# First stage of a LayerNorm, attention and 8-bit FFN kernel: row normalization on ScalarE, score keys on GpSimd, weights loaded once and in four buffers, column maxima after the next statistics

## The reference

```python
x: (4, 512, 512) f32
xn = layernorm(x)                                # over the last axis, no affine part
q = (xn @ wq).reshape(B, T, 32, 16); k = xn @ wk; v = xn @ wv      # one key and one value head of 16
probs = softmax(causal(q k^T / 4)); s = (probs @ v).reshape(B, T, 512) @ wo
h = linear8bit(xn, W1, b1); g = silu(linear8bit(h, W2, b2))
return x + s * g
# linear8bit: columns of x whose absolute maximum is over 3.0 go through a float product,
# the others through a product of int8-quantized rows of x and of W
```

## Time and profile before

| | us |
|---|---|
| median of 3 runs | 842.08 |
| lowest and highest | 839.84 and 845.34 |
| the profiled execution | 841.47 |
| span in its trace | 839.6 |
| PE busy | 772.8 (92%) |
| DVE busy | 664.5 (79%) |
| ACT busy | 402.7 (48%) |
| POOL busy | 255.0 (30%) |

### The profile page before, as it was taken

The page is one execution under the profiler, slowest core; times in us unless marked ns, Lnnn a source line. Parts: engine busy times, 40 slices in busy tenths (PEclk is TensorE's granted clock), DMA queues, the critical chain, the costliest instruction groups (busy, mean ns, idle before and its releaser), DMA issues. The chain is left out here.

```text
span 839.6 us, 12084 instructions
## 1 busy us (share of the span) xinstructions
PE 772.8 (92%) x4253; PEld 581.5 (69%) x4253; DVE 664.5 (79%) x1132; ACT 402.7 (48%) x682; POOL 255.0 (30%) x331
## 2 busy tenths in 40 slices
PE   2899899999999999998879999999987999998982
PEld 2687665556676676665668788787866888886772
DVE  6888899999999999885355665856469998599967
ACT  2123156676776677777424455454444332242321
POOL 7100225555555555553511011101000000136306
PEclk9999789999999999999999999999999999999997
DMA  5731212233322233335244525112005254025852
GB/s 142 248 110 51 50 40 68 81 84 80 103 79 79 81 99 89 89 105 165 77 149 153 193 96 201 45 32 87 26 12 190 62 163 126 25 78 167 273 184 100
DMA packets 53884, 89.90 MB, mean 107 GB/s; under 512 B 10288, under 2 KB 18496, under 8 KB 52416
## 3 DMA queue, kind: packets, MB, share of 16 engines
q1 hardware_dynamic: 53824, 89.13, 33.9%
HBM read 47.69 MB, written 28.31 MB: 91 GB/s over the span
## 5 line engine op out<-in xcount | busy, mean ns | idle before, releaser
L849 DVE TENSOR_REDUCE rowmax<-ps 128x2 f32<-128x512 f32 (+3 forms) x384 | 210.0, 589 | 19.7 <-PE ps L912 17.9
L773 ACT ACTIVATE probs<-ps 128x512 f32<-128x512 f32 (+1 forms) x352 | 174.6, 558 | 71.0 <-PE ps L925 69.4
L912 PE MATMUL ps<-km,stack 128*128 128x256 f32 (+3 forms) x512 | 149.7, 347 | 2.2 <-PEq L171 1.9
L925 PE MATMUL ps<-stack,ks 128*128 128x512 f32 (+1 forms) x352 | 131.6, 383 | 2.7 <-ACT probs L773 2.6
L912 PEld LDWEIGHTS ps<-km,stack 128*128 128x128 f32 (+1 forms) x512 | 94.4, 198 | 43.2 <-DVE rowmax L849 23.7
L1651 PE MATMUL ps<-big_h 128*128 128x512 f32 x256 | 101.0, 394 | 10.2 <-DVE big_l L1576 10.1
L1323 PE MATMUL ps<-big_h,w1h 128*128 128x512 f32 x256 | 105.0, 410 | 1.4 <-DVE w1l L1195 1.4
L755 POOL TENSOR_SCALAR_AFFINE_SELECT probs<-probs 128x512 f32<-128x512 f32 x128 | 80.6, 638 | 78.7 <-ACT probs L773 77.6
L1325 PE MATMUL ps<-big_h,w1l 128*128 128x512 f32 x256 | 101.6, 397 | 0.0
L1324 PE MATMUL ps<-big_l,w1h 128*128 128x512 f32 x256 | 101.3, 396 | 0.0
L1652 PE MATMUL ps<-big_l,big_h 128*128 128x512 f32 x256 | 100.4, 392 | 0.0
(11 more groups left out here) (194 smaller groups left out, 1303.1 us busy)
## 6 DMA issues: line engine op xcount, KB each, us to landing
stack<-big_h SPq DMA_DIRECT2D x128, 64.0 KB, 2.0
projected_rows<-w2t_scratch SPq DMA_DIRECT2D x32, 256.0 KB, 2.7
h_scratch<-hs SPq DMA_DIRECT2D x7, 1024.0 KB, 4.5
hload<-h_scratch SPq DMA_DIRECT2D x14, 512.0 KB, 4.8
xn_scratch<-xa SPq DMA_DIRECT2D x4, 1024.0 KB, 4.3
stack<-big_l SPq DMA_DIRECT2D x64, 64.0 KB, 2.0
xi<-xn_scratch SPq DMA_DIRECT2D x16, 256.0 KB, 2.7
xe_scratch<-xm SPq DMA_DIRECT2D x16, 256.0 KB, 2.3
```

Source lines behind the costliest of these rows:

```text
L773: nc.scalar.activation(probs[p][:, o:o + nh * w], ps[:, STB[n % NST], 0:nh * w], ACT.Exp).then_inc(s_exp, 1)
L849: nc.vector.tensor_reduce(dst, src, AX_X, ALU.max).then_inc(s_red, 1)
L912: last = nc.tensor.matmul(dst, stack[u % 3][rows, hp, P * qt:P * (qt + 1)], km[rows, u // KT, p0:p0 + npar, keys], start=True, stop=True)
L925: ins = nc.tensor.matmul(ps[:, STB[n % NST], 0:nh * w].rearrange("p (h q) -> p h q", h=nh), ks[:, u // KT, p, P * kt:P * (kt + 1)], stack[ ...
```

## The change

- ACT, not DVE, normalizes the rows of groups 1 to 3: `normalize(g+1)` is four activations `x * rstd + shift` of 128x512 behind the two copies of kv(g); DVE forms `shift = -mean * rstd` (128x4). Group 0 stays on DVE, with a signal for each tile, and PE transposes tile by tile.
- POOL, not DVE, forms `ks`: two additions of 128x512 for a group, in front of the spare rows of `km`.
- `wk` and `wv` are loaded once; ACT and DVE read `wk` six times over. Only the 16 zero columns are written by POOL.
- `wq` is loaded in four DMAs of 128x512 into four tiles that are free then, not into `xa`. SP loads group 1 right behind it and waits for nothing.
- The column maxima of group g stand behind `layernorm(g+1)` on DVE. The low parts have their own semaphore `s_tl`, on which PE's kv waits; the maxima free the banks (`s_paf`).
- q(g,1) and q(g,2) stand in front of t(g+1).

```diff
-            if g + 1 < B:
-                a_order += [("q", g, k) for k in range(1, KT)] + [("v", g, 0)]
+                a_order += [("q", g, k) for k in range(1, 3)]
                 a_order += [("t", g + 1, k) for k in range(KT)]
+                a_order += [("q", g, k) for k in range(3, KT)] + [("v", g, 0)]
...
# SP
-                sp.wait_ge(s_wkvz, 1)
-                for c in range(6):
-                    sp.dma_start(wkv_in[:, :, HD * c:HD * (c + 1)],
-                                 wk.rearrange("(k p) n -> p k n", p=P)).then_inc(s_wload["wkv"], 16)
...
-                sp.dma_start(wq_in, wq.rearrange("(k p) n -> p k n", p=P)).then_inc(s_wload["wq"], 16)
-                sp.wait_ge(s_wl, 2)
+                sp.dma_start(wk_in[:, :, :], wk.rearrange("(k p) n -> p k n", p=P)).then_inc(s_wload["wkv"], 16)
+                sp.dma_start(wv_in[:, :, :], wv.rearrange("(k p) n -> p k n", p=P)).then_inc(s_wload["wkv"], 16)
+                for k in range(KT):
+                    sp.dma_start(wq_in[k], wq[P * k:P * (k + 1), :]).then_inc(s_wq[k], 16)
                 load_rows(1)
...
# POOL
+                    for p in range(2):
+                        nc.gpsimd.tensor_tensor(ks[:, g, p, :], km[:, g, p, :].bitcast(F32),
+                                                cols[:, 4 + p:5 + p].broadcast_to([P, T]), ALU.add).then_inc(s_ks, 1)
+                    pool.wait_ge(s_ks, 2 * (g + 1))
...
# ACT
+                def normalize(g):
+                    act.wait_ge(s_sh, g)
+                    for i in range(QT * g, QT * (g + 1)):
+                        rows = xa[:, i % (2 * QT), :]
+                        nc.scalar.activation(rows, rows, ACT.Identity, bias=shift[:, i:i + 1],
+                                             scale=rstd[:, i:i + 1]).then_inc(s_xn, 1)
...
                         nc.scalar.copy(kvh.bitcast(F32R), ps[:, n % 8, :]).then_inc(s_pah, 1)
+                        if g + 1 < B:
+                            normalize(g + 1)
...
# DVE
-                        nc.vector.tensor_reduce(colmax[:, k, g:g + 1], ps[:, n % 8, :], AX_X, ALU.max,
-                                                apply_absolute_value=True)
...
+                        if k == KT - 1:
+                            if g + 1 < B:
+                                layernorm(g + 1)
+                            for j in range(KT):
+                                nc.vector.tensor_reduce(colmax[:, j, g:g + 1], ps[:, a_at[("t", g, j)] % 8, :], AX_X,
+                                                        ALU.max, apply_absolute_value=True).then_inc(s_paf, 1)
...
-                            ins = nc.vector.tensor_scalar(ks[:, g, p, :], km[:, g, p, :].bitcast(F32),
-                                                          cols[:, 4 + p:5 + p], None, ALU.add)
```

More of the change, by code:

```diff
@@ L110, in block_layernorm_attention_ffn @@
         nt_ = sp_("newton", [P, NT])
+        shift = sp_("shift", [P, NT])
         colmax = sp_("colmax", [P, KT, B])
@@ L121, in block_layernorm_attention_ffn @@
         s_x = [sem(f"x_loaded{g}") for g in range(B)]
-        s_wload = {n: sem(f"{n}_loaded") for n in ("wq", "wo", "wkv", "b1")}
+        s_wload = {n: sem(f"{n}_loaded") for n in ("wo", "wkv", "b1")}
+        s_wq = [sem(f"wq_loaded{k}") for k in range(KT)]
         s_wkvz = sem("wkv_zeroed")
@@ L287, in _ @@
                 deviation(0)
[L288 to L291, removed]
+                act.wait_ge(s_wload["wkv"], 16 * 2)
+                nc.scalar.copy(keys_of(wkvh), repeated(wk_in)).then_inc(s_wh, 1)
+                nc.scalar.copy(wkvh[:, :, 7 * HD:P], wv_in[:, :, :]).then_inc(s_wh, 1)
+                for k in range(KT):
+                    act.wait_ge(s_wq[k], 16)
+                    nc.scalar.copy(wqh[:, k, :], wq_in[k]).then_inc(s_wh, 1)
                 for kind, g, k in a_order:
@@ L340, in layernorm @@
                     step(nc.vector.tensor_tensor(rstd[:, r], rstd[:, r], nt_[:, r], ALU.mult))
[L341 to L344, removed]
+                    if g:
+                        nc.vector.scalar_tensor_tensor(out=shift[:, r], in0=mv[:, r, 0], scalar=-1.0, in1=rstd[:, r],
+                                                       op0=ALU.mult, op1=ALU.mult).then_inc(s_sh, 1)
+                    else:
+                        for i in range(QT):
+                            nc.vector.tensor_scalar(xa[:, i, :], xa[:, i, :], mv[:, i, 0:1], rstd[:, i:i + 1],
+                                                    ALU.subtract, ALU.mult).then_inc(s_xn, 1)
                 def weight_low(dst, src, hi, n):
@@ L355, in _ @@
                 layernorm(0)
-                weight_low(wkvl[:, :, :], wkv_in[:, :, :], wkvh[:, :, :], 1)
-                weight_low(wql[:, :, :], wq_in, wqh[:, :, :], 2)
+                weight_low(keys_of(wkvl), repeated(wk_in), keys_of(wkvh), 1)
+                weight_low(wkvl[:, :, 7 * HD:P], wv_in[:, :, :], wkvh[:, :, 7 * HD:P], 2)
+                for k in range(KT):
+                    weight_low(wql[:, k, :], wq_in[k], wqh[:, k, :], 3 + k)
                 for kind, g, k in a_order:
@@ L379, in _ @@
                                                          ALU.mult))
[L380 to L383, removed]
-                            ins = nc.vector.tensor_scalar(ks[:, g, p, :], km[:, g, p, :].bitcast(F32),
-                                                          cols[:, 4 + p:5 + p], None, ALU.add)
+                            ins = nc.vector.scalar_tensor_tensor(out=km[:, g, p, :], in0=kvl,
+                                                                 scalar=cols[:, 2 + p:3 + p],
+                                                                 in1=km[:, g, p, :].bitcast(F32),
+                                                                 op0=ALU.mult, op1=ALU.add)
                         ins.then_inc(s_paf, 1)
@@ L425, in three @@
                         if ready is not None:
-                            pe.wait_ge(s_paf, ready + k)
+                            pe.wait_ge(s_tl, ready + k)
                         nc.tensor.matmul(dst, lh(k), rh(k), start=(k == 0), stop=False)
@@ L435, in _ @@
                     if kind == "t":
+                        if g == 0:
+                            if k:
+                                continue
+                            for j in range(QT):
+                                pe.wait_ge(s_xn, j + 1)
+                                for f in range(KT):
+                                    last = nc.tensor.transpose(ps[:, f, P * j:P * (j + 1)], xa[:, j, P * f:P * (f + 1)],
+                                                               ident[:, :])
+                                    if j == QT - 1:
+                                        last.then_inc(s_pa, 1)
+                            continue
                         if k == 0:
-                            pe.wait_ge(s_xn, g + 1)
+                            pe.wait_ge(s_xn, QT * (g + 1))
                         for j in range(QT):
```

36 lines of the change are left out of this document (23 added, 13 removed).

## The result

| | before | changed |
|---|---|---|
| median of 4 runs each, us | 841.39 | 831.53 |
| lowest and highest | 839.84 and 845.34 | 828.53 and 832.86 |
| the profiled execution | 841.47 | 830.80 |
| its span | 839.6 | 829.0 |
| first row maximum of the second stage (DVE) | 94.51 | 81.77 |

The ratio to the kernel before is 0.9863, 95% interval 0.9835 to 0.989: faster by 1.4%. In a second series (6 runs of the changed kernel, 10 of the one before) it was 0.9851, interval 0.9817 to 0.9886. The forecast was 829.7 with a range of 825.5 to 836.

What follows compares the result with a forecast made beforehand. The first stage was taken as bound by DVE. Gains of 3.8 + 4.2 + 1.4 + 2.4 = 11.8 us off the profiled 841.47 gave 829.7 us, range 825.5 to 836.

Steps and rivals of the forecast that it cites:

- What bounds the kernel: First stage, some 94 us: bound by DVE, whose list costs 18.92 us a group where PE needs 15.86.
- Part 1, the start: Start of the first stage: kv(0) starts at 14.7 and not 18.51, 3.8 us gained, bounds 1.8 and 4.5.
- Part 2, the pause: PE's wait at 30.61 before t(1): 4.2 us go whole, and 1.4 more since PE's clock doesn't fall.
- The clock coming up earlier: Upside in kv(0): PE's clock rises earlier, up to 2.4 us, of which 2 counted, giving 827.7.
- Part 3, the steady state: Later groups of the first stage: DVE takes 16.5 us a group; PE's waits of 1.43 and 1.01 go, 2.4 us.
- the first rival: DVE and ACT's loop stays the bound, activations 0.8 us apiece, t(2) and t(3) wait: 833 us, chance 0.15.
- Part 4: Work given to POOL and ACT: nothing on the path, 0 to 1 us for what stands behind it.
- two rivals with a low clock within the stage: First stage, PE at half speed: 17.4 us long gives 838 (chance 0.08); 40 us gives 848, slower (0.04).
- the gain hidden later: Next stage waits for something that doesn't come earlier, so the whole stays at 841 us; chance 0.05.

Runs made afterwards that it cites:

- first profile: Changed kernel, its first profiled execution, full-speed start: 73.40 us from first normalized tile to first row maximum (85.36 before), span 829.0 us.
- second profile: The same changed kernel profiled again, nothing edited, half-speed start: 72.56 us from first normalized tile to first row maximum, span 828.0 us.

## Why the prediction was right, step by step

- **What bounds the kernel** held for the kernel before: what the loads took off DVE's list arrived at the end (3.7 us), and the reorder of PE's work gave nothing as long as that list was the bound. In the changed kernel DVE and PE are so close that it depends on the execution: the keys showed with their full length (3.2 us), the three normalizations with 2.6 of 5.5 us. One thing the reading left out: both distances, 18.92 and 16.35, hold 1.2 us in which DVE itself waits for ACT's two copies of kv, which ACT begins only when DVE has copied the values of the group before. No run took that out; without it DVE's list would be near 15.1 us (16.35 - 1.22, an estimate), under PE's 15.86. The rows, before and after:

```profile
49.40 0.69 DVE L376 TENSOR_TENSOR w1t_first<-projected_rows 128x512 f32<-128x512 f32 x1 [1.20 <-ACT projected_rows L305]
```

```profile
40.21 0.69 DVE L411 TENSOR_TENSOR w1t_first<-projected_rows 128x512 f32<-128x512 f32 x1 [1.22 <-ACT projected_rows L330]
```

- **Part 1, the start**, 3.8 us: kv(0) started 4.5 us earlier, of which 0.8 came from tiles of x that landed earlier in that execution. From the first normalized tile to kv(0) it is 9.36 before (18.51 - 9.15) and 5.67 after: 3.7. The loads give 3.1 of that (6.27 with them alone), the maxima behind the low parts 0.6 (6.27 again with them undone).
- **Part 2, the pause**, 4.2 + 1.4 us: it went whole. The rows of group 1 were ready at 23.2 (forecast 23.7). t(1) came at 25.01 and not 28.0 in the first profile, since kv(0) started 0.7 us earlier than forecast and ran at full speed from its first matmul (0.47 us, against 0.77); in the second profile, with the half-speed start, it came at 27.98.
- **The clock coming up earlier**, counted as up to 2 us on the good side, was worth nothing. The changed kernel was profiled with both: first part 73.40 with the full-speed start and 72.56 with the half-speed one. PE's gain was given back in front of the queries, t(2) and t(3) (0.38, 0.28, 0.89, 0.29 us), because DVE and ACT were the slower ones then. And the 0.84 us by which the full-speed start came out longer are POOL's copy: it held a DVE instruction for 1.5 us in the first profile (2.00 and not 0.49) and for 0.7 in the second (1.40 and not 0.68), and from the first tile to the statistics of group 2 it was 22.97 and 22.19 us. With the half-speed start the view marks no wait at all after the start of kv(0), and only t(3) came 0.3 us late (16.13 us behind t(2)):

```profile
15.27 0.77 PE L460 MATMUL ps<-xth,wkvh 128*128 128x512 f32 x1 [1.33 <-DVE xtl L396]
```

  This is the last row of that kernel's PE timeline that has a wait, until the second stage.
- **Part 3, the steady state**, 2.4 us: the waits of 1.43 and 1.01 went. In the first profile 1.8 us of new waits took their place, which the sum had at nothing; there the first 24 matmuls took 5.5 us and not 7.8, which it had at nothing either. That its 12.0 us meet the forecast's 11.8 is therefore partly luck; in the second profile the waits stayed away as forecast. 16.5 a group measured 16.35. An activation costs 811 ns alone and 0.71 apart (2.94 us for four); I had 0.65, from a row with a scale alone. The Trainium skill ("ScalarE: Activation LUTs", What ACT_TABLE_LOAD costs) has a fixed part that grows with each operand of one value a row, and an estimate from its figures, for two such operands and 512 elements, is 799 ns and 0.71 apart; the trace agrees, and I should have taken it as a bound. But that is only 0.2 us for four. The waits for ACT came from PE being early: the rows of t(2) were ready at 43.0, near the forecast's 42.7, and PE wanted them at 42.25 and not at 43.7. So the first rival, whose condition was 0.8 apiece, came true in its mechanism only in 1.2 us of pauses for ACT (0.89 and 0.29) with the full-speed start, of which 0.3 were left with the half-speed one; its price of 3.4 us was too high.
- **Part 4**, POOL: 1.04 us an addition where I took 1.28 to 2.24, and no one waited. What I had put at 0 to 1 us, contention with POOL, did cost DVE 1.5 and 0.7 us in the two profiles, but by an old instruction, the copy of the spare rows, which had fallen into DVE's wait for the rows of group 1 before.
- **The clock at the changes of stage**: I took the later stages as a constant. They scatter by 5 us over the twelve traces, more than any term of the sum.
- The sum of 11.8 stands against 12.0 in the first part and 12.8 against its second profile; in whole runs the medians differ by 9.9 and by 13.4 us in the two series.
- The two rivals with a low clock within the stage, and the gain hidden later, are out: the granted clock was 1.00 from 14 to 80 us, and the rest (747.2 and 745.8) isn't longer than 745.1 beyond its scatter.

```profile
14.00:80.20 66.20, 63.61 (x309) 51.76 (x309) 58.58 (x125) 29.50 (x53) 21.26 (x41) 1.00 0.32 110
```

## What to carry to other kernels

Where two engines are nearly full, compare the length of one round in each one's own list (here 18.92 against 15.86 us), not their busy shares; the longer list is the one to take work from, and a new order on the shorter gives nothing yet. Look also for waits inside the longer round. Worths of edits don't add up: the same order of products was worth nothing before and 5.8 us after, so undo parts from the changed kernel as well as trying them alone. When an experiment lands on a rival's number, follow the time through the timeline before you give the rival the mechanism; here an instruction on a third engine had eaten the difference. To weigh parts of some microseconds in a kernel of 840, measure between two events within the trace that every version has, and take the changed kernel's profile twice.

## What was not expected of the hardware

- A VectorE instruction that starts while GpSimd's copy of 32x2048 runs is held until about its end, whatever its own size: 1.82 us for a `tensor_tensor` of 128x4 that takes 0.16 (loads alone), 1.64 for one of 128x512 that takes 0.68 (order undone), 2.00 for a `tensor_scalar` that takes 0.49 (changed). The three ended 0.0, 0.6 and 0.3 us after the copy. Five more traces have the same, with 0.7 to 1.7 us more than usual; in the two with the copy moved, and with the normalization undone, where four `tensor_reduce` from PSUM ran beside it in their usual 2.48 us, nothing was longer. It goes the other way too: a GpSimd instruction of 128x1 that otherwise takes 0.18 us took 3.40 while VectorE formed the low parts of the weights from two tiles in SBUF (10.19 to 13.2, changed):

```profile
9.93 3.40 POOL L245 TENSOR_SCALAR_AFFINE_SELECT band<-band 128x1 f32<-128x1 f32 x1
```

  The Trainium skill ("GPSIMD Engine Reference", Specifications) says that the two engines share their SBUF interfaces and that VectorE instructions with two SBUF inputs or in a two-port mode contend. The trace agrees for the `tensor_tensor` instructions, which have two SBUF inputs; in which mode the `tensor_scalar` ran, no row shows.
- Two executions of one program started kv(0) at full and at half speed (0.47 and 0.77 us for the first matmul, the next ones 0.23 and 0.43 apart), 1.4 and 1.3 us behind the same transposes; the granted clock is recorded as 1.00 in both.
- In two executions of the changed kernel TensorE had its low clock for 13.6 and 7.2 us around the same change of stage (3.2 before). The part behind the first stage took 744.2 to 749.4 us over the twelve traces.
